# A local-attention kernel on one core: the reciprocal roots' inputs and Newton products move from SBUF to the half of a PSUM tensor that the output projection uses

## What is computed

```python
def attn_layer(x, Wqkv, qs, ksc, Wo):          # x: (2, 1024, 128), 16 heads of 64
    q, k, v = split(x @ Wqkv)
    q = l2norm(q) * qs                          # l2norm(t) = t / max(|t|, 1e-12), per head
    k = l2norm(k) * ksc
    q = q * cos * scale + rotate_half(q) * sin * scale
    k = k * cos / scale + rotate_half(k) * sin / scale
    out = local_attention(q, k, v)              # windows of 32 queries, 64 keys, softmax
    return out @ Wo
def ffn_layer(x, g, bln, W1, b1, W2, b2):
    xn = (x - mean) / sqrt(var + 1e-05) * g + bln
    a, gate = split(xn @ W1 + b1)
    return a * gelu(gate) @ W2 + b2
for i in range(6):
    x = attn_layer(shift_tokens(x), ...) + x
    x = ffn_layer(shift_tokens(x), ...) + x
```

## Time and profile before

| | |
|---|---|
| median of 3 runs | 1858.31 us (1854.05 to 1860.98) |
| the profiled execution | 1854.16 us |
| its span, first to last instruction | 1852.3 us |
| mean granted TensorE clock | 0.972 of full speed |
| PE busy | 1673.8 us (90%) |
| DVE busy | 1562.0 us (84%) |
| ACT busy | 1219.1 us (66%) |
| POOL busy | 1488.4 us (80%) |

### The profile page before, as it was taken

One profiled execution on the slowest core, in us unless ns is written; L12 is line 12 of the kernel. 1 busy time (PEld: TensorE's weight loads), 2 busy tenths in 40 slices (PEclk: granted clock), 3 DMA queues, 4 the chain that ended last, 5 costly groups with the idle time before them and its releaser, 6 DMA issues. The chain is left out here.

```text
span 1852.3 us, 76505 instructions
## 1 busy us (share of the span) xinstructions
PE 1673.8 (90%) x30992; PEld 1195.4 (65%) x30992; DVE 1562.0 (84%) x2309; ACT 1219.1 (66%) x2072; POOL 1488.4 (80%) x823
## 2 busy tenths in 40 slices
PE   4957889899999999999999999999999999999985
PEld 3634566667667666676676676676666766766664
DVE  6878667898898898988989989988889989899853
ACT  3435455677777767767677777777677676777754
POOL 3568777788888888888888888888888888888851
PEclk7979889999999999999999999999999999999999
DMA  4002132121332221332212232222242223222220
GB/s 136 1 13 57 48 92 60 47 68 45 81 105 75 54 60 48 94 96 68 68 50 67 75 103 55 68 67 66 67 106 59 54 68 79 57 68 68 58 57 23
DMA packets 80697, 121.87 MB, mean 66 GB/s; under 512 B 16776, under 2 KB 29574, under 8 KB 79750
## 3 DMA queue, kind: packets, MB, share of 16 engines
q1 hardware_dynamic: 80646, 121.14, 24.9%
HBM read 19.36 MB, written 1.05 MB: 11 GB/s over the span
## 5 line engine op out<-in xcount | busy, mean ns | idle before, releaser
L781 PE MATMUL r<-wqkv,xs 128*128 (+1 forms) x1152 | 560.7, 618 | 13.4 <-DVE rot_sin L1298 4.3
L1484 POOL TENSOR_TENSOR rot<-rot,root 128x1024 f32<-128x1024 f32 x192 | 377.7, 1987 | 120.6 <-DVE root L1336 120.6
L1456 POOL TENSOR_TENSOR rot<-rot,rot_sin 128x1024 f32<-128x1024 f32 x192 | 451.8, 2364 | 1.6 <-DVE rot_sin L1298 1.6
L781 PEld LDWEIGHTS r<-wqkv,xs 128*128 128x128 f32 x1152 | 210.0, 195 | 213.4 <-issue 197.7
L1131 ACT ACTIVATE squares<-r 128x512 f32<-128x512 f32 x384 | 217.6, 598 | 80.5 <-PE r L781 79.3
L1287 DVE TENSOR_TENSOR rot<-r,table 128x1024 f32<-128x1024 f32 x192 | 232.8, 1213 | 21.0 <-PE r L786 9.6
L1469 POOL TENSOR_TENSOR squares<-squares 128x512 f32<-128x512 f32 x192 | 244.5, 1273 | 6.6 <-ACT squares L1131 6.5
L1500 POOL TENSOR_TENSOR probs<-probs,rinv 128x1024 f32<-128x1024 f32 x96 | 182.7, 1903 | 81.2 <-DVE rinv L1358 81.2
L1298 DVE TENSOR_TENSOR rot_sin<-r,table 128x512 f32<-128x512 f32 x384 | 242.6, 673 | 0.0
L786 PE MATMUL r<-square,rot 128*128 128x128 f32 x1536 | 208.4, 279 | 17.3 <-POOL rot L1484 11.8
L786 PEld LDWEIGHTS r<-square,rot 128*128 128x128 f32 x1536 | 169.5, 141 | 81.2 <-issue 27.5
(11 more groups left out here) (123 smaller groups left out, 2723.2 us busy)
## 6 DMA issues: line engine op xcount, KB each, us to landing
vwin<-vtok SPq DMA_DIRECT2D x576, 128.0 KB, 2.3
vwin<-vtok SPq DMA_DIRECT2D x384, 64.0 KB, 2.0
wqkv<-in_wqkv SPq DMA_DIRECT2D x6, 1536.0 KB, 8.3
wo<-in_wo SPq DMA_DIRECT2D x6, 512.0 KB, 4.9
w<-in_w SPq DMA_DIRECT2D x6, 341.0 KB, 2.9
x<-in_x SPq DMA_DIRECT2D x4, 256.0 KB, 3.6
rope<-in_rope SPq DMA_DIRECT2D x1, 1024.0 KB
out_x<-y SPq DMA_DIRECT2D x4, 256.0 KB, 2.3
```

The lines of the kernel that those rows point to most:

```text
L781: pe.matmul(dst[:, c * 512:(c + 1) * 512], xs1[:, u, :], w.rearrange("p a n -> p (a n)"), start=True, stop=True).then_inc(S[done], 1)
L1456: pool.tensor_tensor(r, r, rot_sin[:, k, :, :, :].rearrange("p h a d -> p h (a d)"), ALU.add)\
L1484: pool.tensor_tensor(r, r, bcast(root[:, at:at + HEADS], 2, DH), ALU.mult)\
```

## The change

`minus_half` and `root_t` become columns 0 to 66 and 67 to 133 of `pm_out`. `root` and `ss` stay in SBUF. As TensorE writes `pm_out` too, it now waits, ahead of `ff_up(m-4, 1)` and ahead of `out_project(m-2)`, for the whole chain of roots of step m-1. In the other direction, the chain must not begin before `ff_center`'s result has been read out of `pm_out`; so L1313 now stands behind the wait for `var_done`, which was that of L1318 alone.

```diff
-        minus_half = sb("minus_half", [P, ROOTS])
-        root_t = sb("root_t", [P, ROOTS])
         root = sb("root", [P, ROOTS])
...
         pm_norm, pm_out = pm[:, 0:512], pm[:, 512:1024]
+
+        minus_half, root_t = pm_out[:, 0:ROOTS], pm_out[:, ROOTS:2 * ROOTS]
...
                         pe.wait_ge(S["xc_squared"], m - 3)
+                    pe.wait_ge(S["refined"], ROOT_OPS * (min(m, PAIRS + LAG) if isinstance(m, int) else m))
                     ff_up(m - 4, 1, pm_out)
...
                         pe.wait_ge(S["residual1"], m - 3)
+                    pe.wait_ge(S["refined"], ROOT_OPS * (min(m, PAIRS + LAG) if isinstance(m, int) else m))
                     out_project(m - 2)
...
             def find_roots(m):
 
                 before = ROOT_OPS * m
+
                 if runs(m):
                     dve.wait_ge(S["q_summed"], 2 * (m + 1))
                     dve.wait_ge(S["k_summed"], 2 * (m + 1))
-                    dve.tensor_scalar(minus_half[:, 0:QK_ROOTS + 1], ss[:, :],
-                                      1e-24, -0.5, ALU.max, ALU.mult)\
-                       .then_inc(S["refined"], 1 if runs(m - LAG) else 2)
                 if runs(m - LAG):
                     dve.wait_ge(S["var_done"], m - LAG + 1)
+                dve.tensor_scalar(minus_half[:, 0:QK_ROOTS + 1], ss[:, :],
+                                  1e-24, -0.5, ALU.max, ALU.mult)\
+                   .then_inc(S["refined"], 1 if runs(m - LAG) else 2)
+                if runs(m - LAG):
                     dve.tensor_scalar(minus_half[:, QK_ROOTS + 1:ROOTS], pm_norm[:, 0:2], 1e-5, -0.5, ALU.add, ALU.mult)\
-                       .then_inc(S["refined"], 1 if runs(m) else 2)
+                       .then_inc(S["refined"], 1)
```

## The result

The changed kernel takes 1748.44 us (median of 4 runs, 1747.47 to 1751.01), the kernel before 1856.18 in the same comparison: a ratio of 0.942, 95% interval 0.939 to 0.945. The sign and the mechanism on VectorE were as forecast. The size was not: the bound that was set, that the gain is at most the waits that TensorE's rows show, did not hold, and most of what follows is about the 32 us that were missed.

A forecast was written before the change was run, and what follows sets the result against it. TensorE was taken to set the pace, nearly, its idle time bounding the gain. 43 steps at 1.53 us (65.8) plus 10.0 in the fill gave 76 off 1854.2; adjusted towards the median, 1780 us, range 1764 to 1802.

The forecast's parts named there:

- (a): The guess, L1326, reads PSUM and takes 0.20 us instead of 2.21, saving 2.0 us of the chain.
- (b): The first input, L1313, writes PSUM from SBUF: 0.23 us taken instead of 1.10, saving 0.87.
- (c): The nine Newton instructions now run while GpSimd adds; with one input in PSUM they should not stand still.
- (e): L1313 now waits for the variance too, which PE makes "a second early": cost nothing.
- (f): PE's two new waits come 5 us or more after the roots: cost nothing.
- The fill: Steps 0 to 4, before the steady steps: PE's waits there shrink, saving 10.0 us together.
- (d): PSUM's price for the chain's small reads and writes: nothing taken, 1.3 us a step kept for the range.
- so the up projection starts at once: PE gains 0.28 + 1.24 = 1.52 us: Steady step: PE's waits at the down projection (0.28) and for the new x (1.24) vanish.
- more than full: Rival: PE's stretches shrink too, as transposes held by late rotations pack closer; below 1764 us, chance 0.05.
- slack 0.9 or more everywhere: After the change, GpSimd's scaled q and the rotation come 0.9 us or more before PE wants them.

The follow-up runs named there:

- product_in_sbuf: The changed kernel with root_t back in SBUF and only minus_half in PSUM: 1827.99 us, ratio 0.982.
- before_waits_only: The kernel before, all operands in SBUF, with only TensorE's two new waits and the changed order of waits before the first input: 1860.69 us, ratio 1.002.
- before_4_newton: The kernel before with 4 Newton steps instead of 3 in each chain of roots: 1924.4 us.
- changed_6_newton: The changed kernel with 6 Newton steps instead of 3 in each chain of roots: 1843.4 us.

## Why the prediction was right and where it was wrong

**Right.** (a) The guess stood still for GpSimd's addition: 2.21 us to 0.23, and 0.196 without PSUM when no addition runs. (b) So did the first input, 1.10 to 0.23. (c) The Newton products would have stood still in SBUF, and don't in PSUM. The rule of the Trainium skill's page "SBUF — State Buffer", section "Who interferes with whom", is borne out where these runs touch it: an instruction with two SBUF inputs contends (2.27 us for L1341 of product_in_sbuf), one with a single SBUF input and its other side in PSUM does not (0.228 to 0.236). (e) and (f): the moved wait and the two new ones cost nothing in a steady step (before_waits_only, 34.12 us). The "second early" of (e) is a microsecond: 1018.64 less 1017.67. The fill gave 11.2 us in steps 0 to 3 where 8.5 were forecast, and 0.8 in step 4 where 1.5 was.

One reading was too wide: "the instructions that never stand still are those with a side in PSUM". VectorE's sums of squares read one tensor in SBUF and write SBUF, 188 of the 192 of them wholly beside an instruction of GpSimd, and they never stand still either (columns as in the earlier trace rows):

```profile
L1304 DVE TENSOR_REDUCE ss<-squares x192: 627/673/687, 130.3 to 1769.0; 128x16 f32<-128x512 f32 x192
```

So among the instructions with one input, what is shown to stand still from SBUF to SBUF are the two TENSOR_SCALAR forms of the chain, not every instruction.

**(d), PSUM's price.** I took nothing and kept 1.3 us; it is 0.09, without the first input. The Trainium skill's page "VectorE: DVE Perf Modes", section on the TRN2 errata, would have had 0.65, as an estimate, and does not hold for these instructions. For the guess the whole difference, 33 ns, is what 67 elements at 1.06 ns would lose if it went from two elements a cycle to one (35 ns): worked out, not shown.

**Wrong: "so the up projection starts at once: PE gains 0.28 + 1.24 = 1.52 us ... the step becomes 32.6 us, with PE idle 0.3".** The two waits were sized by the idle time in TensorE's rows, and a gain from the chain was held to be "worth at most what PE waits for it". It was 2.30 us, more than all of the 1.86 that TensorE's rows show as idle in a step; so the low end of the range, 1764, which took that whole idle time as gone, was 16 us too high as well. Of the missing 0.77, 0.17 + 0.08 was in the same two waits (1.41 and 0.36 by starts), and 0.10 in the up projection's own row behind one of them. Some 0.06 was in the wait for the scaled q and 0.31 in that for the rotation, which had no listed idle time on TensorE (the last 0.05 is in the groups behind). The rotation's wait I had even used, as "PE's second transposes, which waited for it", and then reckoned with it as a deadline only, and not as a gain. Over 43 steps this is 31 of the 32 us (97 against 65.8). The rival "more than full", with a chance of 0.05, named a part of the right thing ("transposes held by late rotations pack closer"), without working out a number; of the 0.77 it holds the 0.31, while some 0.35 sit in the two waits that had been counted.

**Wrong with it: "slack 0.9 or more everywhere".** It is 0.50, measured. The deadlines had been set from a TensorE that was 1.5 us earlier than before at each point; at the second transposes it is 2.2 earlier (0.36 - 0.01 + 1.41 + 0.16 + 0.31).

## What to carry to other kernels

Look at the spread of a short VectorE instruction's duration: 0.195 to 2.287 us for one shape is not work. Here it was standing still for GpSimd, and it could be taken out by giving the instruction a side in PSUM, once every instruction with two SBUF inputs that then falls under GpSimd's work gets one too. Size a stall on TensorE by the distance between the starts of its groups, set against the same distance where nothing waits, and look at the weight loads' waits; TensorE's own idle time left out the first 0.1 to 0.2 us of each wait here. And count a wait on a second engine's late result as a gain as well as a deadline when the thing that made it late is removed.

## What the runs showed of the hardware that was not expected

**A wait of some 2 us can cost TensorE more than itself.** In before_4_newton the wait for the new x is 2.04 us. In most steps nothing else happens. In 17 of the 41 from step 6 on the granted clock falls to half (1.2 GHz instead of 2.4) when TensorE goes on, as these windows of one such step show (columns as in the earlier trace rows), and the step takes 36.15 us instead of 34.92:

```profile
632.00:634.00 2.00, 0.39 (x2) 0.37 (x3) 1.45 (x5) 0.21 (x1) 1.33 (x1) 1.00 0.55 131
634.00:636.00 2.00, 2.00 (x10) 1.68 (x9) 2.00 (x2) 0.00 (x0) 2.00 (x2) 0.60 0.46 132
636.00:638.00 2.00, 2.00 (x6) 1.12 (x6) 2.00 (x3) 1.25 (x2) 2.00 (x2) 0.54 0.00 0
638.00:640.00 2.00, 2.00 (x13) 1.45 (x12) 1.62 (x4) 1.41 (x4) 2.00 (x3) 1.00 0.00 0
```

Its matmuls there, the 8 transposes, take 1.91 us instead of 1.09. From 556.20 to 1832.63 us, 36 steps of which 14 are such, this cost 1276.4 less 36 x 34.92 = 19 us, most of the 28 that before_4_newton lost beyond the forecast. In the kernel before (idle 1.24) and in changed_6_newton (1.20) no 5 us window between 450 and 1700 us is below 0.95. Why one step falls and the next does not stays open.

Both kernels meet the lower clock in the fill and in the drain too, where TensorE has waits of this size: from 120 to 300 us the granted clock is 0.87 in the kernel before and 0.88 in the changed one, and neither meets it in the steady steps behind. In the drain the same output projection runs into it in both. These are the rows of the kernel before,

```profile
1791.80 0.45 PE L814 MATMUL r<-kT,qT 64*32 64x64 f32 x28 [1.92 <-issue]
1792.18 5.41 PE L839 MATMUL pm<-attnT,wo 128*128 128x256 f32 x16
```

and these of the changed one:

```profile
1684.63 0.68 PE L814 MATMUL r<-kT,qT 64*32 64x64 f32 x32 [1.94 <-issue]
1685.25 6.49 PE L839 MATMUL pm<-attnT,wo 128*128 128x256 f32 x16
```

It takes 3.62 us at full clock, 5.41 and 6.49 here. The difference of the two is not what makes the end later, for the next transposes start 29.06 us behind the chain of step 47 before (1798.88) and 28.26 after (1691.99). The 3 us come later, in the last feed-forward parts, where the changed kernel meets the lower clock twice,

```profile
1714.00:1722.00 8.00, 7.01 (x18) 4.62 (x18) 3.54 (x13) 1.84 (x4) 0.00 (x0) 0.57 0.00 0
1725.00:1733.00 8.00, 6.82 (x17) 4.33 (x15) 1.52 (x4) 2.98 (x6) 0.00 (x0) 0.57 0.01 2
```

and the kernel before once, and shorter:

```profile
1820.00:1828.00 8.00, 6.03 (x20) 4.15 (x20) 3.77 (x14) 2.74 (x6) 0.00 (x0) 0.79 0.01 2
1829.00:1837.00 8.00, 5.57 (x24) 3.76 (x25) 2.35 (x5) 5.24 (x9) 0.00 (x0) 1.00 0.00 0
```

Counted from the start of the chain of step 47, the up projections before the last still start 0.5 us earlier in the changed kernel (at 53.21 us against 53.70), the last down projection 3.0 later (at 69.79 against 66.83). Three groups make the difference: 5.14 us against 4.25, 2.35 against 1.56, and 5.08 against 3.32 for the last up projections. Why the clock falls more often there in this execution is not shown.

**GpSimd's instructions leave gaps.** A VectorE instruction with two SBUF inputs that comes at the seam of two GpSimd instructions passes (0.228 us), and one 0.26 us later waits 2.04. Which instruction of a chain stands still depends on one to three tenths of a microsecond.
